# Second query tile's exponentials ahead of the first tile's fp16 copy, in a fused gated cross-attention and expert kernel

## The chip, the cores and the metric

One core of one Trainium2 chip runs the whole program. The metric is the device time of that core in microseconds. Before the change its median over 3 runs is 476.14 us (475.67 to 477.45).

## The reference

The program computes one transformer block over `x` (8 batches, 256 tokens, 128 channels) and a context of 512 tokens per batch. First comes a gated cross-attention with 16 heads of 64 channels:

```python
q = (xn @ w_q).reshape(B, SQ, NUM_HEADS, DIM_HEAD)
kv = context @ w_kv
scores = jnp.einsum('bqhd,bkhd->bhqk', q * SCALE, k)
attn = jax.nn.softmax(scores, axis=-1)
out = jnp.einsum('bhqk,bkhd->bqhd', attn, v).reshape(B, SQ, INNER)
x = x + jnp.tanh(g_xattn[0]) * (out @ w_out + b_out) * jnp.tanh(gate[0])
```

Then each token goes to the likeliest of 8 experts (at most 160 tokens each), which is a two-layer network of width 512 with a ReLU, and its output is added with a second gate. All inputs and outputs are float32.

## The kernel before

The attention is worked through in 64 steps, one for each batch `b` and pair of heads `hp` (8 batches of 8 pairs; `j = 8*b + hp` counts them). Heads of a pair lie side by side: a score bank holds 128 queries by two heads of 512 keys. The index `qt` (0 or 1) is the tile of 128 queries of the pair. `psAB` holds the scores of `qt` 0, `psCD` those of `qt` 1. There is one bank pair for each, used again by the next pair.

Every engine has its own program, written out in order; semaphores tie them. Nothing reorders the work at run time. For one pair the data goes this way:

- TensorE writes the scores of `qt` 0 and `qt` 1 (`scores`, lines 1234 and 1241). `scores(j, qt)` waits for the exponentials of pair `j-1` of the same `qt`, which free the bank.
- VectorE takes the row maximum of each tile (`row_max`, line 903) and makes of it the bias `NB` (line 906).
- ScalarE takes the exponentials (`exps`, line 752; two instructions, one for each head) from PSUM to the float32 tile `P32`.
- ScalarE copies `P32` to fp16, the high half of a split of each value in two (`phi`, line 762), into `PARTS`.
- GpSimd subtracts the high half from `P32` and writes the low half in fp16 (line 650).
- SyncE issues a DMA transpose of both halves of the tile, `PARTS` to `PT` (line 473), when GpSimd has finished that tile. There are two per pair, one for each `qt`.
- TensorE multiplies the transposed halves with the values of the heads (`values`, lines 1267 to 1269; 48 matmuls, the 24 of `qt` 0 first). It does so two steps later: in step `j` it works on pair `j-2`. VectorE then scales the result (lines 914 and 920).

In step `j` TensorE's order is: the scores of both tiles, the keys and queries of pair `j+2` (lines 1168 to 1170 into `psEF`), the transposes of pair `j-3`'s output (line 1278), what some steps have besides in the bank `psX` (projections, context and token transposes, router logits at line 1294), the values of pair `j-2`, and a block of the values' projection into `psX` (lines 1168 to 1170). That block's high half is copied out by ScalarE (`v_hi`, line 719) and its low half by VectorE (`v_lo`, line 896) in the next step, after the first row maximum; then `psX` is free.

ScalarE's order in a step is the one that the change touches: `exps` of `qt` 0; the copy of the next keys and queries (`kq_hi`, line 714; 3 of 8 steps have none); in single steps a further copy (`xt_copy` line 696 at `hp` 4, `tokt_copy` line 724 at `hp` 5, `v_hi` at `hp` 2); `phi` of `qt` 0; `exps` of `qt` 1; `ot_copy` (line 741); `phi` of `qt` 1; `v_hi`; in single steps a small copy or the router's exponentials.

SyncE's queue also carries loads between the transposes: a batch's context and tokens, 256 KB pieces of the experts' weights at `hp` 3 and 6, and one store of a batch's rows at `hp` 4.

After the 64 steps comes a tail of some 50 us with the last pairs and the experts.

Of the kernel before, what the change touches and what calls it, by code (L numbers as in the profile page):

```python
# [33 lines left out]
def gated_block(nc, x, ctx_1024, g_xattn, g_ffn, ln_gamma, ln_beta, w_q, w_kv, w_out, b_out, gate,  # L34
# [34 lines left out]
    with ExitStack() as ctx:  # L69
# [236 lines left out]
        def slots(b):  # L306

            for hp in range(PAIRS):
                yield b * PAIRS + hp, hp
# [5 lines left out]
        def is_last(b):  # L315
            return isinstance(b, int) and b == B - 1

        def is_first(b):
            return isinstance(b, int) and b == 0
# [6 lines left out]
        def v_group(b, hp):  # L326

            if hp >= PAIRS - 2:
                return None if is_last(b) else (b + 1, 0, hp - PAIRS + 2)
            return (b, 0, hp + 2) if hp < 2 else (b, 1, hp - 2)  # L330
# [4 lines left out]
        def ot_pair(j):  # L335

            return j - OT_BEHIND
# [25 lines left out]
        def next_pair(b, hp, k):  # L363

            return (b, hp + k) if hp + k < PAIRS else (b + 1, hp + k - PAIRS)
# [24 lines left out]
        def score_bank(qt):  # L390

            return psCD if qt else psAB
# [291 lines left out]
        def _(act):  # L684
# [5 lines left out]
            def xt_copy(b):  # L690

                act.wait_ge(xt_psum, b + 1)
                if b:

                    act.wait_ge(xt_lo_done, b)
                act.activation(XS[:], x_bank(b)[:, 0:SQ], ACT.Identity, bias=norm_q[:, 1:2],
                               scale=norm_q[:, 0:1]).then_inc(xt_f32, 1)

            def xt_hi(b):
                act.wait_ge(xt_f32, b + 1)  # L700
                act.activation(xT_hi[:, b % 2, :], XS[:], ACT.Copy).then_inc(xt_hi_done, 1)

            def ctxt_hi(b):
                act.wait_ge(ctxt_psum, b + 1)
                act.activation(cT_hi[:, b % 2, :], psX[:], ACT.Copy).then_inc(ctxt_hi_done, 1)

            def kq_hi(b, hp):
                j = b * PAIRS + hp
                if whole(j):
                    return  # L710
                act.wait_ge(kq_psum, j + 1)
                if ot_pair(j - AHEAD) >= 0:
                    act.wait_ge(ot_psum, ot_pair(j - AHEAD) + 1)
                act.activation(HL[:, hp % 2, H_KHI:H_KHI + KQ], kq_bank(j)[:, 0:KQ], ACT.Copy).then_inc(kq_hi_done, 1)  # L714

            def v_hi(b, half, kt, bank=psX):
                n = b * 2 * KT + half * KT + kt
                act.wait_ge(v_psum, n + 1)
                act.activation(VH[:, kt, 8 * half:8 * half + 8, 0:DH],  # L719
                               bank[:].rearrange("p (h d) -> p h d", d=DH), ACT.Copy).then_inc(v_hi_done, 1)  # L720

            def tokt_copy(b, bank=psX):
                act.wait_ge(tokt_psum, b + 1)
                act.activation(tT[:], bank[:, 0:QT * P], ACT.Copy).then_inc(tokt_done, 1)

            def router_exp(b):
                act.wait_ge(rstd_done, b + 1)
                act.wait_ge(route, b * ROUTE + 2)
                for q in range(QT):
                    last = act.activation(lexp[:, q, :], cand[:, q, :], ACT.Exp, scale=rstd[:, q:q + 1])  # L730
                last.then_inc(lexp_done, 1)

            def ot_copy(n, bank=psOT, pairs=1):

                b, pair = divmod(n, PAIRS)
                act.wait_ge(ot_psum, n + pairs)
                act.wait_ge(kq_done, min(n + OT_BEHIND + AHEAD + 1, LAST + 1))
                if b:

                    act.wait_ge(part_psum if pair < PAIRS // 2 else proj_psum, b)  # L740
                act.activation(OT[:, QT * pair:QT * (pair + pairs), :], bank.rearrange("p (t c) -> p t c", c=P),  # L741
                               ACT.Copy).then_inc(ot_done, pairs)

            def exps(b, hp, qt):
                j = b * PAIRS + hp
                par = hp % 2
                act.wait_ge(bias_done, 2 * j + qt + 1)
                if j >= 2:

                    act.wait_ge(plo_done, 2 * j - 4 + qt + 1)  # L750
                for h in range(2):
                    last = act.activation(P32[:, par, qt, SK * h:SK * h + SK], score_bank(qt)[:, SK * h:SK * h + SK],  # L752
                                          ACT.Exp, bias=NB[:, par, qt, h:h + 1])
                last.then_inc(exp_done, 1)

            def phi(b, hp, qt):
                j = b * PAIRS + hp
                act.wait_ge(exp_done, 2 * j + qt + 1)
                if j >= 2:

                    act.wait_ge(pt_in[qt][hp % 2], transposed_value(j - 2))
                act.activation(PARTS[:, hp % 2, qt, 0], P32[:, hp % 2, qt], ACT.Copy).then_inc(phi_done[qt], 1)  # L762
# [19 lines left out]
            def batch(b):  # L782
                for j, hp in slots(b):
                    if hp == CTX_STEP + 1 and not is_last(b):
                        ctxt_hi(b + 1)
                    exps(b, hp, 0)
                    if not (is_last(b) and hp + AHEAD >= PAIRS):
                        kq_hi(*next_pair(b, hp, AHEAD))
                    if hp == CTX_STEP:
                        v_hi(*v_group(b, hp))  # L790
                    if hp == X_STEP and not is_last(b):
                        xt_copy(b + 1)
                    if hp == TOKT_STEP and not is_first(b):
                        tokt_copy(b - 1)
                    if j < LAST:
                        phi(b, hp, 0)
                    exps(b, hp, 1)
                    if ot_pair(j) >= 0:
                        ot_copy(ot_pair(j))
                    if j < LAST:  # L800
                        phi(b, hp, 1)
                    if hp != CTX_STEP and v_group(b, hp):
                        v_hi(*v_group(b, hp))
                    if hp == X_STEP and not is_last(b):
                        xt_hi(b + 1)
                    if hp == LOGITS_STEP and not is_first(b):
                        router_exp(b - 1)

            each_batch(batch)
            for qt in range(QT):  # L810
                act.wait_ge(p_psum, qt + 1)
# [730 lines left out]
```

## Time and profile before

| | us |
|---|---|
| median of 3 runs | 476.14 |
| the profiled execution, its own time | 477.22 |
| its span | 475.4 |
| PE (TensorE) busy | 437.4 (92%) |
| ACT (ScalarE) busy | 386.3 (81%) |
| DVE (VectorE) busy | 360.6 (76%) |
| POOL (GpSimd) busy | 356.5 (75%) |

The profile shows one execution. Times in it are microseconds from the start of the span. An engine's row gives the start, the duration, the line of the kernel, what is written and read, and in brackets the idle time of the engine before it with what ended it. SPq is the queue of SyncE; a transpose's row there is the time of its issue, not that of its transfer. A row of the windows view gives the stretch, its length, the busy time of PE, PEld (TensorE's weight loads), DVE, ACT and POOL with the count of instructions, TensorE's granted clock, the DMA share and GB/s. A row of landing times gives the least, the median and the most from the issue of a transfer to its landing.

### The profile page before, as it was taken

The page shows a single profiled execution, that of the slowest core. Times are in us where ns is not written, and L with a number is a line of the kernel's source. Part 1 is how long each engine was busy: PE and PEld are TensorE (multiplying, and loading weights), DVE is VectorE, ACT ScalarE, POOL GpSimd, SP SyncE. Part 2 cuts the span into 40 slices and gives each one's busy share as a digit, 9 for nine tenths or more (in the row PEclk, how much of TensorE's full clock was granted, in tenths as well). Part 3 has the DMA queues.
Part 4 walks back from the last instruction along what each step waited for, and adds up shares of the span by engine and source line. Part 5 has one row for each costly group of instructions (what it writes and reads, how often), then busy time and mean ns, then how long its engine had stood idle before and what let it go on. Part 6 is the DMA issues. An engine that isn't in the chain of part 4 may idle for free.

```text
span 475.4 us, 13024 instructions
## 1 busy us (share of the span) xinstructions
PE 437.4 (92%) x5030; PEld 330.3 (69%) x5030; DVE 360.6 (76%) x789; ACT 386.3 (81%) x630; POOL 356.5 (75%) x270
## 2 busy tenths in 40 slices
PE   5789999999999999999999999999999899987793
PEld 3466667776777766776777677767687577766793
DVE  4678887778887897889777888789788777893522
ACT  4789988899988998899889998899889889881230
POOL 3677886888878887898788887888789787851225
PEclk9899999999999999999999999999999999999799
DMA  5399999899999999999999999999999979993201
GB/s 169 147 145 207 213 188 188 170 181 196 194 193 209 193 195 203 168 218 212 188 184 196 200 200 174 212 182 202 186 172 167 185 155 163 146 192 100 58 11 44
DMA packets 283036, 82.08 MB, mean 173 GB/s; under 512 B 264387, under 2 KB 280435, under 8 KB 282976
## 3 DMA queue, kind: packets, MB, share of 16 engines
q1 hardware_dynamic: 281600, 77.96, 93.0%
q0 software_dynamic: 1376, 3.30, 2.1%
q8 instruction: 40, 0.66, 0.6%
q14 instruction: 20, 0.16, 0.1%
HBM read 10.83 MB, written 5.14 MB: 34 GB/s over the span
## 4 chain that ended last, share of the span: by engine, by line
PE 45%; DVE 20%; ACT 15%; issue 8%; DMA 6%; POOL 4%; POOLq 0%; another core or an unknown queue 0%; SPq 0%; ACTq 0%; DVEq 0%
DVE MXL L903 8%; ACT P L752 7%; DMA PT<-PARTS 5%; PE psAB L1234 4%; PE psAB L1241 4%; DVE HL L890 3%; POOL PARTS L650 3%; ACT HL L714 3%; PE psO L1267 3%; PE psX L1319 3%; PE psCD L1241 3%; ACT PARTS L762 3%; PE psO L1269 3%; PE psX L1355 3%; PE psO L1268 3%
## 5 line engine op out<-in xcount | busy, mean ns | idle before, releaser
L650 POOL TENSOR_TENSOR PARTS<-P,PARTS 128x1024 f16<-128x1024 f32 x125 | 267.4, 2144 | 61.1 <-ACT PARTS L762 59.7
L762 ACT ACTIVATE PARTS<-P 128x1024 f16<-128x1024 f32 x126 | 136.0, 1080 | 0.8 <-DMA PT<-PARTS 0.2
L752 ACT ACTIVATE P<-psAB,NB 128x512 f32<-128x512 f32 x128 | 81.6, 694 | 39.2 <-DVE NB L906 38.7
L903 DVE TENSOR_REDUCE MXL<-psAB 128x2 f32<-128x1024 f32 x64 | 78.3, 1224 | 40.4 <-PE psAB L1241 23.2
L1267 PE MATMUL psO<-VH,PT 128*128 128x65 f16 x1008 | 98.4, 194 | 3.8 <-DMA PT<-PARTS 3.1
L1268 PE MATMUL psO<-VL,PT 128*128 128x64 f16 x1008 | 98.3, 192 | 0.0
L1269 PE MATMUL psO<-VH,PT 128*128 128x65 f16 x1008 | 98.2, 193 | 0.0
L1267 PEld LDWEIGHTS psO<-VH,PT 128*128 128x128 f16 x1008 | 92.0, 98 | 7.2 <-DMA PT<-PARTS 3.8
L1268 PEld LDWEIGHTS psO<-VL,PT 128*128 128x128 f16 x1008 | 91.3, 98 | 0.5
L1269 PEld LDWEIGHTS psO<-VH,PT 128*128 128x128 f16 x1008 | 91.4, 97 | 0.0
L752 ACT ACTIVATE P<-psCD,NB 128x512 f32<-128x512 f32 x128 | 81.7, 703 | 0.1
L903 DVE TENSOR_REDUCE MXL<-psCD 128x2 f32<-128x1024 f32 x64 | 77.7, 1214 | 0.2 <-PE psCD L1241 0.2
L896 DVE TENSOR_TENSOR VL<-psX,VH 128x512 f16<-128x512 f32 x63 | 43.1, 684 | 8.7 <-ACT VH L719 8.5
L890 DVE TENSOR_TENSOR HL<-psEF,HL 128x768 fp32r<-128x768 f32 x41 | 39.2, 957 | 7.7 <-ACT HL L714 4.2
L1241 PE MATMUL psCD<-HL 64*128 64x512 f32 x252 | 38.1, 407 | 5.9 <-ACT P L752 5.8
L1241 PE MATMUL psAB<-HL 64*128 64x512 f32 x252 | 41.2, 432 | 2.0 <-ACT P L752 2.0
L719 ACT ACTIVATE VH<-psX 128x512 f16<-128x512 f32 x63 | 39.3, 624 | 0.0
L714 ACT ACTIVATE HL<-psEF 128x768 fp32r<-128x768 f32 x41 | 33.3, 813 | 2.7 <-PE psEF L1170 2.5
L741 ACT ACTIVATE OT<-psEF 128x256 f32<-128x256 f32 (+1 forms) x63 | 26.1, 414 | 11.5 <-PE psEF L1278 8.4
L1168 PEld LDWEIGHTS psEF<-cT_hi,w_hi 128*128 128x128 f32 x63 | 11.9, 189 | 32.8 <-issue 31.1
L1241 PEld LDWEIGHTS psCD<-HL 64*128 64x128 f32 x252 | 23.1, 187 | 16.1 <-ACT P L752 11.7
L1168 PE MATMUL psEF<-cT_hi,w_hi 128*128 128x512 f32 x63 | 32.0, 508 | 1.3 <-DVE cT_lo L877 1.3
(208 smaller groups left out, 865.0 us busy)
## 6 DMA issues: line engine op xcount, KB each, us to landing
ctx_raw<-in_ctx_dram SPq DMA_DIRECT2D x8, 256.0 KB, 3.6
w1s<-in_L_ffn_w_dram SPq DMA_DIRECT2D x8, 256.0 KB, 3.9
w2s<-in_L_ffn_w_dram SPq DMA_DIRECT2D x8, 256.0 KB, 3.5
PT<-PARTS SPq DMA_TRANSPOSE x126, 5.2
experts_table<-zeros POOLq DMA_DIRECT2D x2, 645.0 KB
X<-in_x_dram SPq DMA_DIRECT2D x8, 128.0 KB, 3.0
wraw<-in_L_xattn_w_kv_dram SPq DMA_DIRECT2D x4, 256.0 KB, 4.7
out_dram<-row SPq DMA_DIRECT2D x8, 128.0 KB, 2.7
```

Of the source, the lines that this page charges most:

```text
L650: pool.tensor_tensor(PARTS[:, par, qt, 1], P32[:, par, qt], PARTS[:, par, qt, 0], ALU.subtract).then_inc(plo_done, 1)
L714: act.activation(HL[:, hp % 2, H_KHI:H_KHI + KQ], kq_bank(j)[:, 0:KQ], ACT.Copy).then_inc(kq_hi_done, 1)
L752: last = act.activation(P32[:, par, qt, SK * h:SK * h + SK], score_bank(qt)[:, SK * h:SK * h + SK], ACT.Exp, bias=NB[:, par, qt, h:h + 1])
L762: act.activation(PARTS[:, hp % 2, qt, 0], P32[:, hp % 2, qt], ACT.Copy).then_inc(phi_done[qt], 1)
L890: dve.tensor_tensor(hl[:, H_KLO:H_KLO + KQ], kq_bank(j)[:, 0:KQ], hl[:, H_KHI:H_KHI + KQ].bitcast(F32), ALU.subtract).then_inc(kq_done, 1)
L896: dve.tensor_tensor(VL[:, kt, 8 * half:8 * half + 8, :], bank[:].rearrange("p (h d) -> p h d", d=DH), VH[:, kt, 8 * half:8 * half + 8, 0:D ...
L903: dve.tensor_reduce(MXL[:, par, qt, :, 0], score_bank(qt)[:].rearrange("p (h n) -> p h n", h=2), AX.X, ALU.max, negate=True).then_inc(max_ ...
L1168: pe.matmul(dst, hi_l, hi_r, start=True, stop=False)
L1241: last = pe.matmul(score_bank(qt)[:, SK * h:SK * h + SK], hl[rows, q + P * qt:q + P * qt + P], hl[rows, k:k + SK], start=(q == H_QHI and k ...
L1267: pe.matmul(psO[:, g:g + DH + 1], phi, VH[:, kt, head, 0:DH + 1], start=first_, stop=False)
L1268: pe.matmul(psO[:, g:g + DH], phi, VL[:, kt, head, :], start=False, stop=False)
L1269: last = pe.matmul(psO[:, g:g + DH + 1], plo, VH[:, kt, head, 0:DH + 1], start=False, stop=last_)
```

## The change

In each step but the last, ScalarE's program has `exps` of `qt` 1 ahead of `phi` of `qt` 0, and not behind it. Nothing else is changed: the same instructions with the same operands, semaphores and waits.

```diff
                     if hp == TOKT_STEP and not is_first(b):
                         tokt_copy(b - 1)
+                    exps(b, hp, 1)
                     if j < LAST:
                         phi(b, hp, 0)
-                    exps(b, hp, 1)
                     if ot_pair(j) >= 0:
                         ot_copy(ot_pair(j))
```

## Rows read from the trace of the kernel before

**Rows 1.** The page's busy time, share of span and instructions of each engine.

```profile
PE 437.4 (92%) x5030; PEld 330.3 (69%) x5030; DVE 360.6 (76%) x789; ACT 386.3 (81%) x630; POOL 356.5 (75%) x270
```

**Rows 2.** Busy time by windows: the pair steps, and the fifth batch alone.

```profile
18.00:425.00 407.00, 389.30 (x4623) 287.82 (x4624) 331.40 (x698) 364.63 (x588) 331.99 (x231) 0.99 1.07 189
...
222.90:274.60 51.70, 50.66 (x617) 37.67 (x614) 42.62 (x93) 46.34 (x75) 43.56 (x32) 1.00 1.10 193
```

**Rows 3.** Waits of TensorE's matmuls, 18 to 425 us: total, times, longest.

```profile
PE psCD L1241 <- ACT P L752: 5.8, 11, 1.2
PE psX L1186 <- DVE VL L896: 4.4, 7, 0.7
PE psO L1267 <- DMA PT<-PARTS: 3.1, 6, 1.3
```

**Rows 4.** Waits of all engines, and of SyncE's queue, whole span.

```profile
POOL PARTS L650 <- ACT PARTS L762: 59.7, 83, 3.4
ACT P L752 <- DVE NB L906: 38.7, 41, 2.2
...
SPq L473 <- POOL PARTS L650: 179.9, 90, 17.6
```

**Rows 5.** ScalarE in order of time, fifth batch, pair hp 4.

```profile
251.48 1.07 ACT L762 ACTIVATE PARTS<-P 128x1024 f16<-128x1024 f32 x1
252.43 1.28 ACT L752 ACTIVATE P<-psCD,NB 128x512 f32<-128x512 f32 x2
253.57 0.42 ACT L741 ACTIVATE OT<-psEF 128x256 f32<-128x256 f32 x1
253.83 1.10 ACT L762 ACTIVATE PARTS<-P 128x1024 f16<-128x1024 f32 x1
```

**Rows 6.** VectorE in order of time: the same pair's second bias.

```profile
250.91 0.16 DVE L906 TENSOR_REDUCE NB<-MXL 128x2 f32<-128x4 f32 x1
```

**Rows 7.** GpSimd in order of time: the same pair's two low halves.

```profile
252.64 2.15 POOL L650 TENSOR_TENSOR PARTS<-P,PARTS 128x1024 f16<-128x1024 f32 x1 [1.23 <-ACT PARTS L762]
255.01 2.15 POOL L650 TENSOR_TENSOR PARTS<-P,PARTS 128x1024 f16<-128x1024 f32 x1 [0.23 <-ACT PARTS L762]
```

**Rows 8.** SyncE's queue in order of time, fifth batch, ahead of hp 4's transposes.

```profile
252.05 1.74 SPq L455 DMA_DIRECT2D w2s<-in_L_ffn_w_dram  x2
254.81 5.60 SPq L473 DMA_TRANSPOSE PT<-PARTS  x2
```

**Rows 9.** Line 473: landing of transposes issued 249 to 263.3 us.

```profile
DMA to landing us min/median/max: 4.4/4.4/6.2
```

**Rows 10.** TensorE in order of time: values of hp 4, before and after its second tile's start.

```profile
263.03 0.19 PE L1269 MATMUL psO<-VH,PT 128*128 128x65 f16 x1
263.25 0.20 PE L1267 MATMUL psO<-VH,PT 128*128 128x65 f16 x1
```

**Rows 11.** Line 473 at 211.9 us (fourth batch, hp 5, second tile), and TensorE's first matmul on it.

```profile
L473 SPq DMA_TRANSPOSE PT<-PARTS x1: 3372/3372/3372, 211.9 to 211.9; - x1
...
DMA to landing us min/median/max: 5.3/5.3/5.3
...
217.31 0.19 PE L1267 MATMUL psO<-VH,PT 128*128 128x65 f16 x1
```

**Rows 12.** ScalarE and VectorE in order of time, fifth batch, hp 5 into hp 6.

```profile
256.71 0.45 ACT L724 ACTIVATE tT<-psX 128x256 f32<-128x256 f32 x1
256.97 1.13 ACT L762 ACTIVATE PARTS<-P 128x1024 f16<-128x1024 f32 x1
...
260.27 0.70 ACT L719 ACTIVATE VH<-psX 128x512 f16<-128x512 f32 x1
...
257.31 0.16 DVE L906 TENSOR_REDUCE NB<-MXL 128x2 f32<-128x4 f32 x1
...
261.14 0.68 DVE L896 TENSOR_TENSOR VL<-psX,VH 128x512 f16<-128x512 f32 x1
```

**Rows 13.** TensorE in order of time: router logits of hp 6, fifth batch.

```profile
261.87 0.61 PE L1294 MATMUL psX<-gw_mid,tT 128*128 128x8 f32 x4
```

## The prediction

> **What bounds the kernel now.** I read the busy shares first [rows 1]: PE 92%, ACT 81%, POOL 75%. Then the windows [rows 2]: in the fifth batch, a full turn of eight pairs, PE's matmuls fill 50.66 of 51.70 us with the clock granted in full, while ACT has 5.4 us free and POOL 8.1. So in a steady batch TensorE leaves about 1 us open. The reader is to see that little can be won there, whatever ACT does. Then PE's own waits [rows 3]: of 407 us, 5.8 us in 11 waits are for the exponentials that free `psCD`. 4.4 us are for `v_lo` and 3.1 us for transposed tiles. Last, the other engines' waits [rows 4]: POOL waits 59.7 us in 83 places for the fp16 copy, and SyncE's queue waits 179.9 us in 90 places for POOL (17.6 of it is one wait). So `phi`, the low half, the transpose and the values form a chain with little slack, each link starting when the one before ends.
>
> The Trainium skill (Perfetto Trace Analysis, Identifying the Most-Contended Engine) says that matmul busy time is a poor measure of room on TensorE and that weight-load time is the better one. By that, 37.67 of 51.70 us is taken in the fifth batch and TensorE has room. The waits above disagree: they list almost no time in which it stood.
>
> **What the change adds and removes.** No instruction is added or removed; 63 steps have two neighbours swapped, no DMA and no queue entry moves.
>
> *The gain: earlier `exps` of `qt` 1.* At hp 4 ACT's further copy gives way to `phi` at 251.48 and `exps` starts at 252.43 [rows 5]. Its bias was ready at 250.91 + 0.16 = 251.07 [rows 6]. Swapped, `exps` starts at 251.48, 0.95 us earlier. What it is worth is what PE waits for it: at most 5.8 us [rows 3], about half of it in the first batch, the rest some 0.25 us a batch at one pair and 1.1 us in the last batch. Elsewhere PE is not ready for the scores of `qt` 1 any earlier, so the gain is zero.
>
> *The cost: later `phi` of `qt` 0, and what hangs on it.* `phi` starts after two exponentials. They take 253.57 − 252.43 = 1.14 us from start to the next instruction's start [rows 5], so `phi` moves from 251.48 to 252.62. POOL's first low half was released by `phi` after 1.23 us idle [rows 7], so it moves from 252.64 to 253.78 and ends at 255.93. `phi` of `qt` 1 keeps its time, 253.83, for the sum ahead of it is the same. POOL's second low half started at 255.01; now it can start only at 255.93, and ends at 258.08 instead of 257.16: 0.92 us late. So both tiles are late, the first by 1.14 and the second by 0.92 us, although only one copy moved.
>
> The two transposes are issued from 254.81, when the first low half ends (252.64 + 2.15 = 254.79), and the queue had been free since 252.05 + 1.74 = 253.79 [rows 8]. The lateness passes through: 255.95 and 258.1. They land up to 6.2 us after issue [rows 9]. Now who waits: the values of hp 4 run without a gap to 263.03, and the second tile's first matmul starts at 263.25 instead of 263.06 [rows 10]. PE had already caught up with the transfer: slack zero. At hp 5 of the fourth batch a transpose issued at 211.9 lands 5.3 us later, at 217.2, and is used at 217.31 [rows 11]: slack 0.1. Six waits for transposed tiles in 62 pairs [rows 3] say that most other pairs have theirs in time.
>
> Per batch there is then one delay of the lateness less the slack. Once TensorE is late, the following pairs' scores are late too, so the same microsecond isn't paid twice in that batch, but the next batch pays again, as the lateness is measured from the pair's own scores. The lateness is 1.14 and 0.92 us, so about 1.0. I take all of it for the fifth to seventh batches (slack zero), 0.95 for the fourth, and 0.7 for the second and third, whose slack I put at 0.3 as an estimate above the 0.1 of the fourth: 5.35 us. Bounds of the lateness that reaches PE, per batch: 0, if the transfer engines had a backlog when the transpose came; 1.25, if the second tile is held up as much as the first and its issue comes late besides. I take the value near the top, since the queue was free when the first transpose came [rows 8].
>
> The skill (DMA: Bandwidth & Descriptors, Latency and other measured facts) gives 261 GB/s for one kernel's DMA transposes. An estimate from that page is 2.0 us for a tile of 512 KiB, so two tiles would take 4.0 us of a pair's 6.4 and a late one would be caught up before use. No run here shows that spare time: landing takes 4.4 to 6.2 us [rows 9].
>
> *ACT now waits in three of eight steps.* Where no `kq_hi` stands between (hp 5, 6, 0), the second bias isn't ready when `exps` of `qt` 1 comes. At hp 5 the copy ahead gives way at 256.97, the bias comes at 257.31 + 0.16 = 257.47 [rows 12]. Before, `phi` lay in that gap. Now ACT idles 0.5 us, and `phi` of `qt` 1 and `v_hi` come 0.5 us later: `v_hi` ends at 261.5 rather than 260.97. `v_lo` started at 261.14 [rows 12], now at 261.5, and router logits, which need its bank, started at 261.87 [rows 13], right after it (261.14 + 0.68 = 261.82). They move by 0.35 us. That is a delay ahead of the same values of hp 4, so it is inside the 1.0 us. The same at hp 0, where `ot_copy` was held up anyway, should cost about 0.13 us in each of six batches: 0.8 us. At the end, the last-but-one pair (hp 6) passes its 0.6 us on to the last exponentials and from there to the tail; I take 0.7, between 0 and 0.9.
>
> *First and last batch.* In the first, PE gains near 2 us at its early pairs, but the values there follow the landings by 0.5 to 1 us, and by nothing at hp 4 and 5, so the gain is spent within a few pairs: 0, between −2 and +1. In the last, the gain of 1.1 meets 0.6 of lateness: −0.5. The 0.25 us gained in each middle batch comes just ahead of the wait for the transposed tile and is lost in it: 0.
>
> **Sum.** 5.35 + 0.8 + 0.7 + 0 − 0.5 = 6.35 us. I take a fifth off the 5.35 and the 0.8 for transfers that catch up: 5.1 us. The profiled execution took 477.22 us, so 482.3 in its place. It lies 1.08 above the median of the three runs, so the predicted time is 476.14 + 5.1 = 481.2 us.
>
> **The rivals.**
>
> *Faster: PE's wait is what counts.* Place: the scores of `qt` 1. The 5.8 us [rows 3] go, and the late tiles are caught up because the transfer engines were backlogged when they came. It decides where the lateness that reaches the values stays below the slack plus 0.25 us. For it: the waits are real, and each load of 256 KB ahead of a transpose could hide lateness. Against it: the queue was empty for 1 us before the critical transpose [rows 8], and five of those waits are only 0.25. With 1 to 2 us lost at the tail it gives 476.14 − 4.3 = 471.8. The rule on weight-load time belongs here. Chance 0.10.
>
> *No change.* Transfers absorb all but 0.2 us a batch (1.2), the losses at hp 0 and tail are 1.5, the gains outside the middle batches 2: 476.14 + 0.7 = 476.8. For it: PE waits for a transposed tile only six times before the change [rows 3], and some of the lateness falls into the time in which the queue is loaded anyway. The page's transfer rate would mean this one. Chance 0.23.
>
> *Much slower: ACT or POOL becomes the chain.* The idle stretches of ACT (0.5, 0.6 and 0.9 us at hp 5, 6 and 0) are all passed on, 2.0 us in each of seven batches, beside a part of the above: 476.14 + 14 = 490. Against it: ACT waits 38.7 us for the first bias in 41 places [rows 4], so it has room to catch up, 5.4 us in a batch [rows 2]. Chance 0.09.
>
> **Chances and range.** Forecast 0.58, no change 0.23, faster 0.10, much slower 0.09. The forecast's own range is 478 to 485. To hold 8 in 10 I go to 474.8 below and 485.8 above, which takes most of the no-change case. A measurement of this kernel tells about 0.5% (2.4 us) from nothing. Slower by more than that: 0.09 and nearly all of 0.58, so 0.66; within it 0.23; faster 0.11.
>
> **What would show each step.** In the profile after: PE's waits `psCD` <- ACT nearly gone; ACT idle before `exps` of `qt` 1 at hp 5, 6 and 0 (a new row of waits for the bias, in `psCD`'s form); POOL's two low halves back to back, with no idle before the second; the first transpose issued about 1.1 us later from the pair's first exponentials; PE's waits for the transposed tiles up from 3.1 us to about 8, one at hp 4 or 5 of each batch; a batch of 51.3 to 52.9 us grown by about 1. The prediction is wrong if the landing times, measured from the pair's scores, don't move, or if they move and TensorE doesn't wait. It is wrong in size if waits come at more than one pair of a batch, or if `v_lo` gates TensorE more than the transposes do.

## Result: 2.8% slower, more than twice the forecast loss

The changed kernel takes 489.88 us in the median of 6 runs (487.83 to 494.11); the kernel before, beside it, 476.79 us (475.67 to 480.98). The ratio is 1.0276, 95% interval 1.0239 to 1.0312, so 13.1 us are lost. The forecast was 481.2 us with a range to 485.8: the sign was right, the size wrong.

The profiled execution took 492.89 us with a span of 491.0, against 477.22 and 475.4. First the page's busy line, which answers to [rows 1], then its line on the chain that ended last, by engine.

```profile
PE 436.6 (89%) x5030; PEld 332.8 (68%) x5030; DVE 362.8 (74%) x789; ACT 385.7 (79%) x630; POOL 355.5 (72%) x270
```

```profile
POOL 53%; issue 25%; PE 10%; DMA 5%; ACT 3%; DVE 3%; POOLq 1%; SPq 0%; ACTq 0%; DVEq 0%
```

The same line before:

```profile
PE 45%; DVE 20%; ACT 15%; issue 8%; DMA 6%; POOL 4%; POOLq 0%; another core or an unknown queue 0%; SPq 0%; ACTq 0%; DVEq 0%
```

No instruction was added, and TensorE's busy time even fell from 437.4 to 436.6 us. All of the loss is idle time. Before, TensorE led the chain with 45%; now GpSimd does, with 53%. That share is no measure of the loss: in e5 below, which loses 2.6 us, GpSimd still leads with 39%. TensorE's waits over the whole program, the changed kernel (answer to [rows 3]):

```profile
PE psO L1267 <- DMA PT<-PARTS: 12.3, 16, 1.6
...
PE psX L1186 <- DVE VL L896: 3.9, 6, 0.7
PE psX L1286 <- DVE VL L896: 3.0, 6, 0.5
PE psX L1294 <- DVE VL L896: 3.0, 7, 1.4
PE psX L1333 <- issue: 3.0, 1, 3.0
PE psCD L1241 <- ACT P L752: 2.3, 3, 0.8
PE psX L1319 <- DVE VL L896: 1.8, 6, 0.6
PE psX L1168 <- DVE VL L896: 1.8, 2, 0.9
...
PE psAB L1241 <- ACT P L752: 1.5, 1, 1.5
```

Before, beside the waits of [rows 3]:

```profile
PE psAB L1241 <- ACT P L752: 2.0, 1, 2.0
...
PE psX L1294 <- DVE VL L896: 1.1, 1, 1.1
...
PE psAB L1308 <- ACT P L752: 0.9, 1, 0.9
```

Together they make a balance. Waits for transposed tiles: 3.1 to 12.3, +9.2. Waits for `v_lo`: 4.4 + 1.1 = 5.5 before; now the 13.5 of the five rows above and 1.1 in three smaller ones (L1365, L1302, L1333), 14.6, so +9.1. The ranks (L1333, the places of the tokens within their experts), 0.2 to 3.0, +2.8. Waits for the exponentials (`psCD`, `psAB`): 5.8 + 2.0 + 0.9 and a last one of 0.2 before, 8.9, and 3.8 now, −5.1. Together +16.0, beside 15.6 us of span. So the wait that the change attacks did shrink, and two others grew by more than three times as much.

How one batch grew: ScalarE's first exponentials of the fifth and the sixth batch, first the kernel before, then the changed one.

```profile
221.61 0.69 ACT L752 ACTIVATE P<-psAB,NB 128x512 f32<-128x512 f32 x1
...
273.35 0.69 ACT L752 ACTIVATE P<-psAB,NB 128x512 f32<-128x512 f32 x1
```

```profile
232.41 0.69 ACT L752 ACTIVATE P<-psAB,NB 128x512 f32<-128x512 f32 x1 [0.73 <-DVE NB L906]
...
286.05 0.69 ACT L752 ACTIVATE P<-psAB,NB 128x512 f32<-128x512 f32 x1 [1.50 <-DVE NB L906]
```

51.74 us became 53.64. Read the same way, the seven full batches took 50.0, 51.3, 51.3, 51.3, 51.7, 52.1 and 52.9 before, and 54.9, 53.4, 53.0, 53.0, 53.6, 53.1 and 53.7 after. The six batches in the middle grew by 9.1 us together. From the last batch's hp 6 to the end it was 58.6 and is 60.1. TensorE's waits for transposed tiles in those six batches, before (67.75 to 378.40 us) and then in the changed kernel (73.09 to 392.79 us):

```profile
PE psO L1267 <- DMA PT<-PARTS: 2.1, 4, 1.3
```

```profile
PE psO L1267 <- DMA PT<-PARTS: 7.4, 11, 1.6
```

In the same stretches the waits for `v_lo` went from 3.9 to 10.3 us and those for the exponentials from 1.5 to 0.

Now the pair that the prediction followed, hp 4 of the fifth batch, in the changed kernel: ScalarE, which answers to [rows 5].

```profile
262.21 1.28 ACT L752 ACTIVATE P<-psCD,NB 128x512 f32<-128x512 f32 x2
263.35 1.09 ACT L762 ACTIVATE PARTS<-P 128x1024 f16<-128x1024 f32 x1
264.30 0.42 ACT L741 ACTIVATE OT<-psEF 128x256 f32<-128x256 f32 x1
264.56 1.10 ACT L762 ACTIVATE PARTS<-P 128x1024 f16<-128x1024 f32 x1
```

GpSimd at hp 4 and at hp 5, which answers to [rows 7]:

```profile
264.52 4.24 POOL L650 TENSOR_TENSOR PARTS<-P,PARTS 128x1024 f16<-128x1024 f32 x2 [1.44 <-ACT PARTS L762]
...
270.52 4.24 POOL L650 TENSOR_TENSOR PARTS<-P,PARTS 128x1024 f16<-128x1024 f32 x2 [0.27 <-ACT PARTS L762]
```

The two low halves now stand in one row, back to back. Measured from the pair's own first exponentials (249.19 before, 259.92 after), the first starts 4.60 us in instead of 3.45, and the second ends at 8.84 instead of 7.97: late by 1.15 and 0.87, as worked out. What SyncE's queue makes of it (answer to [rows 8]):

```profile
263.86 1.64 SPq L455 DMA_DIRECT2D w2s<-in_L_ffn_w_dram  x2
266.69 6.32 SPq L473 DMA_TRANSPOSE PT<-PARTS  x2
273.06 0.58 SPq L444 DMA_DIRECT2D out_dram<-row  x1
273.74 5.62 SPq L473 DMA_TRANSPOSE PT<-PARTS  x2
```

The same queue before, in which the last row is hp 5's first transpose:

```profile
260.45 0.58 SPq L444 DMA_DIRECT2D out_dram<-row  x1
261.13 2.87 SPq L473 DMA_TRANSPOSE PT<-PARTS  x1
```

hp 5's first transpose went from 261.13 − 255.57 = 5.56 us after its own exponentials to 273.74 − 266.30 = 7.44: late by 1.88, although GpSimd had its tile only 1.2 late. hp 4's two issues held the queue until 273.01, the store until 273.64. And TensorE, at the second tile of the values of hp 4 and of hp 5 (answer to [rows 10]):

```profile
274.47 0.20 PE L1267 MATMUL psO<-VH,PT 128*128 128x65 f16 x1 [0.19 <-DMA PT<-PARTS]
...
281.74 0.20 PE L1267 MATMUL psO<-VH,PT 128*128 128x65 f16 x1 [1.48 <-DMA PT<-PARTS]
```

The wait forecast at hp 4 is small; the large one is a pair later. The fifth batch is one of the two with the largest wait at hp 5. In the six middle batches the second tile of hp 5 is waited for every time, by 0.40 to 1.64 us, that of hp 4 by 0.19 to 0.39 us in four of the six, and one of hp 6 once. GpSimd delivers both tiles of hp 5 about 1.2 us late in all six; the queue then issues the first 0.7 to 1.9 us late.

### The profile page after: what moved, and what is told of

Its sections match the earlier page's. It is cut to its first block, busy times and chain, and to the rows that moved or that the text cites. A ratio compares the mean times of both kernels' runs of the same rounds, so it can differ in the third digit from the quotient of the medians.

```text
span 491.0 us, 13024 instructions
## 1 busy us (share of the span) xinstructions
PE 436.6 (89%) x5030; PEld 332.8 (68%) x5030; DVE 362.8 (74%) x789; ACT 385.7 (79%) x630; POOL 355.5 (72%) x270
## 3 DMA queue, kind: packets, MB, share of 16 engines
q1 hardware_dynamic: 281600, 77.96, 91.1%
## 4 chain that ended last, share of the span: by engine, by line
POOL 53%; issue 25%; PE 10%; DMA 5%; ACT 3%; DVE 3%; POOLq 1%; SPq 0%; ACTq 0%; DVEq 0%
POOL PARTS L650 41%; DMA PT<-PARTS 4%; POOL XN L543 2%; POOL experts_table L615 2%; PE psEF L1479 2%; POOL row L593 2%; POOL xT_lo L548 1%; POOL X L629 1%; DVE MXL L903 1%; PE psX L1488 1%; PE psO L1488 1%; POOL rstd L588 1%; POOL rstd L536 1%; ACT PARTS L762 1%; ACT P L752 1%
## 5 line engine op out<-in xcount | busy, mean ns | idle before, releaser
L762 ACT ACTIVATE PARTS<-P 128x1024 f16<-128x1024 f32 x126 | 134.4, 1070 | 0.0
L1267 PE MATMUL psO<-VH,PT 128*128 128x65 f16 x1008 | 100.8, 195 | 12.9 <-DMA PT<-PARTS 12.3
L1267 PEld LDWEIGHTS psO<-VH,PT 128*128 128x128 f16 x1008 | 92.8, 99 | 17.6 <-DMA PT<-PARTS 13.2
L1268 PE MATMUL psO<-VL,PT 128*128 128x64 f16 x1008 | 100.6, 193 | 0.0
L1269 PE MATMUL psO<-VH,PT 128*128 128x65 f16 x1008 | 100.5, 194 | 0.0
L752 ACT ACTIVATE P<-psCD,NB 128x512 f32<-128x512 f32 x128 | 81.5, 693 | 16.8 <-DVE NB L906 16.8
L1268 PEld LDWEIGHTS psO<-VL,PT 128*128 128x128 f16 x1008 | 92.3, 99 | 0.5
L1241 PE MATMUL psCD<-HL 64*128 64x512 f32 x252 | 36.3, 392 | 2.3 <-ACT P L752 2.3
L1168 PE MATMUL psX<-w_hi,cT_hi 128*128 128x512 f32 x63 | 30.7, 488 | 2.7 <-DVE VL L896 1.8
L1241 PEld LDWEIGHTS psAB<-HL 64*128 64x128 f32 x252 | 20.5, 185 | 17.0 <-issue 10.3
```

The lines of the kernel that those rows point to most:

```text
L1168: pe.matmul(dst, hi_l, hi_r, start=True, stop=False)
L1241: last = pe.matmul(score_bank(qt)[:, SK * h:SK * h + SK], hl[rows, q + P * qt:q + P * qt + P], hl[rows, k:k + SK], start=(q == H_QHI and k ...
L1267: pe.matmul(psO[:, g:g + DH + 1], phi, VH[:, kt, head, 0:DH + 1], start=first_, stop=False)
L1268: pe.matmul(psO[:, g:g + DH], phi, VL[:, kt, head, :], start=False, stop=False)
L1269: last = pe.matmul(psO[:, g:g + DH + 1], plo, VH[:, kt, head, 0:DH + 1], start=False, stop=last_)
```

## The experiments

Intervals are 95% intervals of the ratio to the kernel before; microseconds lost are the ratio's excess over 1 times 477. Code added to or taken from a kernel shifts its line numbers (the wait at L1267 above stands at L1271 or L1265 below); the tile names tell the rows. A profile shows one execution, so lengths of batches in it are weaker evidence than the ratios.

### The swap in parts

Four kernels have the swap at some pairs only. This is e1's edit of the changed kernel; e2 has `hp not in (4, 5)`, e9 `hp in (2, 3)`, e10 `hp in (6, 7, 0, 1)`:

```diff
-                    exps(b, hp, 1)
+                    early = hp in (4, 5)
+                    if early:
+                        exps(b, hp, 1)
                     if j < LAST:
                         phi(b, hp, 0)
+                    if not early:
+                        exps(b, hp, 1)
```

**e1, hp 4 and 5.** 

> The swap at pairs hp 4 and 5 alone, in all eight batches. Theory A (the late phi of qt 0 makes GpSimd's two low halves, the transposes and so the values of hp 4 and 5 late, and TensorE waits for each of them): it holds what the middle batches lost, 1.3 us each beside most of what the first lost, so 484 to 488 us. Theory B (ScalarE idle before the second bias at hp 5, 6 and 0 is passed on by v_hi and v_lo): only one of its three places is here, so 478 to 480. Theory C (the loss is spread over all pairs): a quarter of it, about 480.

**e2, all but hp 4 and 5.** 

> The swap at all pairs but hp 4 and 5. Theory A: the tiles of the other pairs land 1 us or more before their use and TensorE doesn't wait for them, so the middle batches keep their time; what is left is the first batch's early pairs and the tail (hp 6's late low half holds up the mark of the experts and the ranks), 477 to 480 us. Theory B: two of three idle places are here, 484 or more. Theory C: three quarters of the loss, about 486.

**e9, hp 2 and 3.** 

> The swap at pairs hp 2 and 3 alone. Their own tiles land 1.4 us or more before use, and ScalarE has no idle time before the second bias there. If lateness is carried on by GpSimd, SyncE's queue and the transfers to the next pairs (theory A with carry), the waits appear at hp 4 and 5 and it costs 3 to 6 us: 480 to 483. If each tile is late by itself alone, nothing but the first batch's early pairs is left, 477 to 478.5.

**e10, hp 6, 7, 0 and 1.** 

> The swap at pairs hp 6, 7, 0 and 1 alone. With carry, the lateness of these pairs meets slacks of 1.4 to 6 us at hp 7, 0, 1 and 2 and should be spent there in the middle batches; left are ScalarE's idle time at hp 6 and 0, the first batch's first two pairs and the tail: 3 to 5 us, 480 to 482. If the parts added up to the whole 13 us, with 7.1 at hp 4 and 5, this would be the rest that hp 2 and 3 don't cost.

| swap at | ratio | interval | us lost |
|---|---|---|---|
| e1: hp 4, 5 | 1.0151 | 1.0104 to 1.0197 | 7.2 |
| e9: hp 2, 3 | 1.0099 | 1.0065 to 1.0132 | 4.7 |
| e10: hp 6, 7, 0, 1 | 1.0091 | 1.0055 to 1.0127 | 4.3 |
| e2: all but 4, 5 | 1.0233 | 1.0158 to 1.0307 | 11.1 |
| all | 1.0276 | 1.0239 to 1.0312 | 13.2 |

No group of pairs is free. The parts don't simply add up: e1, e9 and e10 make 16.2 us together, e1 and e2 18.3 (give or take 4), where the whole swap costs 13.2, so some of the cost seems to be shared. e1's time fits the theory of late tiles, but its waits don't single them out:

```profile
PE psO L1271 <- DMA PT<-PARTS: 5.7, 11, 2.2
```

That is 2.6 us more than before, while its waits for `v_lo` are 11.7 against 5.5. e2 flatly contradicts the theory's first form: pairs whose tiles land with time to spare cost 11 us. e10's time is as expected, but not its account: its waits for tiles are 9.0 us, at hp 4 to 6 but for one of 2.1 in the first batch, so the lateness isn't all spent in the slack. e9 shows why. Its waits of TensorE:

```profile
PE psO L1271 <- DMA PT<-PARTS: 9.3, 12, 1.8
```

They stand at hp 4 to 6 for the most part, where this kernel's order is the old one. In its sixth batch hp 4's low half of qt 0 is in time on GpSimd:

```profile
307.95 2.14 POOL L650 TENSOR_TENSOR PARTS<-P,PARTS 128x1024 f16<-128x1024 f32 x1 [0.28 <-ACT PARTS L762]
```

SyncE's queue there, and then TensorE's start on hp 5's second tile:

```profile
303.57 5.63 SPq L473 DMA_TRANSPOSE PT<-PARTS  x2
309.24 1.58 SPq L455 DMA_DIRECT2D w2s<-in_L_ffn_w_dram  x2
310.92 7.06 SPq L473 DMA_TRANSPOSE PT<-PARTS  x2
...
318.71 10.64 SPq L473 DMA_TRANSPOSE PT<-PARTS  x4
```

```profile
327.47 0.20 PE L1271 MATMUL psO<-VH,PT 128*128 128x65 f16 x1 [1.85 <-DMA PT<-PARTS]
```

Compare the kernel before at the same place, GpSimd and then SyncE's queue:

```profile
304.24 2.15 POOL L650 TENSOR_TENSOR PARTS<-P,PARTS 128x1024 f16<-128x1024 f32 x1 [1.23 <-ACT PARTS L762]
```

```profile
304.38 1.58 SPq L455 DMA_DIRECT2D w2s<-in_L_ffn_w_dram  x2
306.41 6.07 SPq L473 DMA_TRANSPOSE PT<-PARTS  x2
...
313.20 8.51 SPq L473 DMA_TRANSPOSE PT<-PARTS  x3
```

The low half ends 5.6 us after the pair's first exponentials in both (304.50 and 300.79). But its transpose is issued 5.62 us after them before, when the low half ends, and 6.42 in e9, when hp 3's late transposes and the loads behind them have left the queue. One pair on it is 6.03 before (313.20 − 307.17) and 7.83 in e9 (318.71 − 310.88). Lateness passes down the queue, and grows there. This batch shows the largest case. At hp 4 of the six middle batches the kernel before issues the first transpose 0.03 us after its low half each time; e9 does so 0.2 to 0.8 us after it in five of them, and in the seventh batch, where the queue has fewer loads, at once.

### Only the first batch, and all but the last

**e3, the swap where `j < PAIRS`.** 

> The swap in the first batch alone. By the two profiles the first batch is 4.9 us longer after the change, which I had put at 0: if that comes from the swap in it, 480 to 482 us. If it came from where the granted clock happened to fall in that profile, the time is within 1 us of before, 476 to 478.

479.23 us, ratio 1.0040 (1.0010 to 1.0069): 1.9 us, between the two expectations. Its profiled first batch took 54.9 us like the changed kernel's. But in e14 below, whose order in the first batch is that of the kernel before, that batch took 51.5 in its profile, not 50.0, and in e7 51.9. With the swap in it the profiles have 54.9, 54.9, 54.0, 54.0 and 51.9 (changed kernel, e3, e11, e13, e6). One profile doesn't hold the first batch's length to better than 2 to 3 us; the means are 51.1 and 53.9.

**e11, the swap where `b < B - 1`.** 

> The swap in all batches but the last. The tail of the profile after was 1.5 us longer than before: GpSimd's late low half of the last but one pair holds up the marking of the experts, the ranks on TensorE and with them the last transposes. If that is the swap's doing, 1.5 to 3 us come back: 487 to 488.5. Otherwise it stays at 489 to 490.

489.77 us, ratio 1.0255 (1.0194 to 1.0315): 1.0 us came back in the ratio, whose interval is 2.9 us to either side. Inconclusive for the tail. The wait of 3.0 us for the ranks (L1333) is gone from its list, so that wait is the swap's doing. The profiles of the other runs say more. From the last batch's hp 6 to the end, kernels whose last batch has the order of the kernel before take 57.0 (e1), 56.3 (e3), 57.1 (e4), 56.7 (e7), 57.0 (e8), 57.5 (e9), 57.3 (e11) and 57.0 us (e12); the 58.6 of the kernel before is the longest of them. With the swap there it is 60.1 (changed kernel), 60.9 (e2), 59.2 (e10) and 59.0 (e6). The tail costs some 2.5 to 3 us, an estimate from these profiles, and not the 1.5 of the first pair of them.

### Late tiles without touching ScalarE, and ScalarE's order without late tiles

**e4, one added instruction on GpSimd.** 

> The kernel before, ScalarE's order untouched, with one added GpSimd instruction of about 1.1 us (a sum of 448 columns into a spare tile) ahead of the low half of qt 0 at hp 4 and 5. It makes the transposed tiles as late as the swap does there (1.1 and 0.9 us) and leaves ScalarE alone. Theory A: near the time of the swap at hp 4 and 5 alone, 483 to 487 us. Theory B: no loss, 476 to 478.

```diff
...
+                        if qt == 0 and hp in (4, 5):
+                            if b or hp > 4:
+                                pool.wait_ge(spare_done, 2 * b + hp - 4)
+                            pool.tensor_tensor(spare[:, 0:448], P32[:, par, qt, 0:448], P32[:, par, qt, 0:448],
+                                               ALU.add).then_inc(spare_done, 1)
                         pool.tensor_tensor(PARTS[:, par, qt, 1], P32[:, par, qt], PARTS[:, par, qt, 0],
                                            ALU.subtract).then_inc(plo_done, 1)
```

The lines left out make the spare tile and its semaphore. 482.96 us, ratio 1.0101 (1.0065 to 1.0136): 4.8 us, just under the range of theory A. Lateness of the tiles alone, with ScalarE as before, costs two thirds of what the swap costs at the same pairs (e1, 7.2). Its waits:

```profile
PE psO L1274 <- DMA PT<-PARTS: 10.9, 13, 1.9
```

**e5, the changed kernel with a shorter low half.** 

> The changed kernel, with GpSimd's low half of qt 0 made for the first head of the pair only (512 of 1024 columns; the second head's low half of that tile is left at zero, so that part of the computation is left out). The GpSimd instruction then takes about 1.1 us instead of 2.1 and the tile is as early as before the change, ScalarE's order stays the changed one. Theory A (late tiles, carried on by GpSimd and SyncE's queue): most of the loss is gone, 477 to 481 us. Theory B (ScalarE idle before the second bias, passed on by v_hi and v_lo): the loss stays, 487 to 490.

```diff
...
+                        n = 2 * SK if qt else SK
-                        pool.tensor_tensor(PARTS[:, par, qt, 1], P32[:, par, qt], PARTS[:, par, qt, 0],
+                        pool.tensor_tensor(PARTS[:, par, qt, 1, 0:n], P32[:, par, qt, 0:n], PARTS[:, par, qt, 0, 0:n],
                                            ALU.subtract).then_inc(plo_done, 1)
...
```

The lines left out have VectorE set the unused low half to zero at the start. 480.24 us, ratio 1.0054 (1.0018 to 1.0090): 2.6 us are left of 13.2. GpSimd's two low halves of hp 4 in the fifth batch, and then ScalarE's first exponentials of that pair:

```profile
255.26 3.36 POOL L654 TENSOR_TENSOR PARTS<-P,PARTS 128x512 f16<-128x512 f32 x2 [2.33 <-ACT PARTS L766]
```

```profile
250.65 1.27 ACT L756 ACTIVATE P<-psAB,NB 128x512 f32<-128x512 f32 x2 [1.50 <-DVE NB L910]
```

The second low half ends 258.62 − 250.65 = 7.97 us in, the figure of the kernel before to the hundredth. ScalarE's order is the changed one. Its waits:

```profile
PE psO L1272 <- DMA PT<-PARTS: 5.3, 10, 1.1
PE psX L1191 <- DVE VL L900: 4.4, 7, 0.7
PE psX L1291 <- DVE VL L900: 3.3, 7, 0.5
PE psX L1299 <- DVE VL L900: 3.1, 7, 1.4
...
PE psX L1324 <- DVE VL L900: 1.8, 6, 0.6
```

The waits for `v_lo` are all still there, as in the changed kernel (14.7 us in all, against its 14.6). The 2.6 us (0.9 to 4.3) are what they cost less what the shorter waits for the exponentials give back. So about 10.6 of the 13.2 us hang on late tiles. This is the run that decides between the theories. Two things it doesn't separate. The edit also takes about 1 us of work from GpSimd in every pair, and the kernel before wasn't run with that same edit at all pairs (e12 has it at four of eight). And in the six middle batches alone the split is more even: they are 3.8 us longer than before in e5's profile, 9.1 in the changed kernel's.

### Is it the loads in the queue?

**e6 and e7, the experts' loads moved**, in the changed kernel and in the one before.

```diff
-        PIECES = {3: 2, 6: 1}
+        PIECES = {0: 0, 1: 1, 7: 2}
...
```

> The changed kernel, with the 256 KB loads of the experts' weights moved in SyncE's queue from hp 3 (two) and 6 (one) to hp 0, 1 and 7 (one each), where the transposes have slack. If lateness is carried from pair to pair by a queue that has no room from hp 3 to hp 6 (theory D), 3 to 6 us come back: 484 to 487. If each tile is late by itself alone (theory A without the queue), the waits at hp 4 and 5 stay and it is 488 to 490.

> The kernel before with the same loads moved. It has 3.2 us of waits for transposed tiles, most of them in the sixth and seventh batches; theory D says that they go and it is 473 to 476 us. Without theory D it is within 1 us of before, 476 to 478.

e6: 488.41 us, ratio 1.0264 (1.0171 to 1.0357). e7: 477.37 us, 1.0004 (0.9971 to 1.0037). No gain can be told in either, though e6's interval is too wide to rule out the 3 us of its expectation. In e6 the waits for tiles are 11.2 us in 20 places; they moved, in part to hp 0 to 3, at and behind the places where the loads now are.

**e13 and e14, the loads taken out of the pair steps** and issued behind them, in the changed kernel and in the one before.

> The changed kernel with all sixteen 256 KB loads of the experts' weights taken out of the pair steps and issued after them, ahead of the experts (which adds some 10 to 20 us of waiting to the tail, the same as in the kernel before with the same edit). What counts is the difference to that kernel. If the transfer queue's lack of room carries the lateness from pair to pair, the difference shrinks from 13 us to 8 or less and the waits for transposed tiles in the middle batches fall from about 1.4 us a batch to under 0.7. If GpSimd's two low halves in a row carry it, the difference stays at 11 to 14.

> The kernel before with the same edit, as the base for the last one. Its waits for transposed tiles (3.1 us, in the last batches with loads) go to near 0 if the loads make them, so its pair steps take 2 to 3 us less; its time as a whole is 485 to 495 for the later loads.

e13: 498.49 us, 1.0419 (1.0353 to 1.0484). e14: 487.32 us, 1.0200 (1.0144 to 1.0255). The difference of the medians is 11.2 us. Their waits for tiles, e13 first:

```profile
PE psO L1265 <- DMA PT<-PARTS: 8.1, 12, 1.8
```

```profile
PE psO L1265 <- DMA PT<-PARTS: 3.7, 5, 1.4
```

Without the loads the swap adds 4.4 us of these waits, with them 9.2. So about half of the added waits go with the loads. But the difference in time shrank by only 2 us of 13, at the edge of what these runs tell, so my expectation of 8 or less failed, and so did that of under 0.7 us of these waits in a middle batch (it is 0.8). The waits for `v_lo` are as long as in the changed kernel (14.5 us). The waits in the sixth and seventh batches did not go in e14 either (they are 2.9 of its 3.7 us), so the loads don't make them. In the kernel before, it is the landing that is long there: the second tile of hp 5 lands 6.0 and 6.4 us after its issue, against 4.6 to 5.3 in the four batches ahead. What makes it long is open.

One rival stays untested. By the profiles' pages, the packets of the queue that these transfers go through take 93.0% of the 16 transfer engines' span before and 91.1% after. Whether an issue holds the queue long by itself, or because the transfer engines behind it are busy, no run here separates.

### The other direction

**e8, the copy of keys and queries behind `phi` of `qt` 0 at hp 4 and 7**, in the kernel before: `phi` comes 0.7 us earlier.

```diff
-                    if not (is_last(b) and hp + AHEAD >= PAIRS):
+                    later = hp in (4, 7)
+                    ahead = not (is_last(b) and hp + AHEAD >= PAIRS)
+                    if ahead and not later:
                         kq_hi(*next_pair(b, hp, AHEAD))
...
                     if j < LAST:
                         phi(b, hp, 0)
+                    if ahead and later:
+                        kq_hi(*next_pair(b, hp, AHEAD))
                     exps(b, hp, 1)
```

> The kernel before with ScalarE's copy of the next keys and queries behind phi of qt 0 at hp 4 and 7 instead of ahead of it: the opposite of the change, phi of qt 0 comes 0.7 us earlier there. Theory A: the tiles of hp 4 and, through the queue, of hp 5 land 0.5 to 0.7 us earlier and the waits for them shrink, 473.5 to 476 us. Against it: the copy's low half on VectorE waits 0.9 us longer and holds up the scaling of the output, then 477 to 479.

480.52 us, ratio 1.0054 (1.0022 to 1.0087): slower by 2.6 us. Waits for tiles fell from 3.1 to 2.3 us, and those for the exponentials rose from 5.8 to 8.9 at line 1241 of the kernel before. The waits for `v_lo`, which VectorE makes, rose as well, from 5.5 to 7.5. The counter-argument of the expectation held, by its sign; whether by the scaling of the output, as it says, I didn't trace.

**e12, the kernel before with the low half of `qt` 0 at hp 2 to 5 made for one head only.** 

> The kernel before, with GpSimd's low half of qt 0 at hp 2, 3, 4 and 5 made for the first head of the pair only (the second head's low half keeps what an earlier pair left, so that part of the computation is left out). The tiles come 1 us earlier than before. The reverse of the change's effect: if the time hangs on the tiles' lateness alike in both directions, 3 us are won at most, since that is all that TensorE waits for them: 474 to 476. If nothing moves, TensorE's own work is the bound in the kernel before.

475.29 us, ratio 0.9978 (0.9944 to 1.0012): no difference that can be told. Its waits for tiles are 4.3 us, not fewer than the 3.1 before. The run makes only the first tile of a pair early; the low half of the second, for which TensorE mostly waits, ends when it did (7.97 us after the first exponentials at hp 4). So it says that an earlier first tile wins nothing sure, and nothing of an earlier second one. Tiles 1 us later lose 5 to 10 us (e4, and e5 against the changed kernel). No version here beats the kernel before for certain.

## Why the prediction was wrong in size

**Right: what moves, and by how much.** `exps` of `qt` 1 earlier, `phi` late by 1.14, the low halves late by 1.14 and 0.92, back to back: the trace has 1.15 and 0.87. The idle time of ScalarE before the second bias at hp 5 came too, and `v_lo` made the logits of hp 6 late. The waits for the exponentials shrank by 5.1 us, and as forecast the gain was lost again, though at another place: TensorE, early at hp 5, waits 0.5 us for `v_lo` before the token transposes (L1286, in each of six batches), not for the tile.

**Right in its sum, partly by luck: the late tiles of the middle batches.** The term was 5.35 us for six batches, and the waits for tiles there grew from 2.1 to 7.4, by 5.3. The swap at hp 4 and 5 alone (e1) makes these batches 5.9 us longer in its profile. But the term had one delay of 1.0 us, at hp 4 of the fifth batch, and 0.7 in the second and third for a slack that was guessed. The waits stand mostly at hp 5, whose two tiles come 1.2 us late from GpSimd and then find a queue that hp 4's tiles and the store still hold: 1.88 us late at issue in the fifth batch.

**Failed: the other pairs' lateness put at nothing.** That "most other pairs have theirs in time" was the step, read from six waits for transposed tiles before. I took it as a sign that lateness elsewhere is spent in the slack between landing and use. e9 and e2 show that it isn't: it leaves the pair by the queue, not by the tile, and what I called hidden was hidden only for the pair itself. The six middle batches grew by 9.1 us, where the sum had 5.35 + 0.8, and 4.9 after the discount. "The same microsecond isn't paid twice in that batch" holds in part: e1 and e2 cost more one by one (18.3 us) than together (13.2), a difference just clear of their intervals. But the following pairs don't just shift along.

**Failed: 0 for the first batch.** e3 has 1.9 us there (0.5 to 3.3). Its middle lies outside the bound of +1, its interval doesn't.

**Mis-sized: the tail and `v_lo`.** For the tail I had 0.7; the profiles of the runs put it at some 2.5 to 3 us. Nothing was put down for the ranks: at the last batch's hp 6, `phi` comes after 0.92 us of ScalarE's idle time and the exponentials of `qt` 1, GpSimd marks the experts behind that tile's low half, and TensorE stands 3.0 us. `v_lo` at hp 0 and 1 was put at 0.13 us a batch; the wait at L1319 is up to 0.6. The waits for it before were 5.5 us, not the 4.4 of the one row that I read, and over the program they now exceed those for tiles (14.6 against 12.3). That was one of the signs named for an error in size; waits at more than one pair of a batch was the other, and it came too.

**The rivals.** The time is that of "much slower" (490), its mechanism isn't. That rival passed ScalarE's idle time on, and e5, which keeps it (17.6 us before the second exponentials, 16.8 in the changed kernel), loses 2.6 us, not 13. "No change" counted on the same slack, and its chance of 0.23 was too high. The discount for "transfers that catch up" had the wrong sign.

**Room on TensorE.** The "faster" rival gave the waits for the exponentials their worth and had the late tiles caught up. It fell: 5.1 us less of such waits went with 13 us more in all. The Trainium skill (Perfetto Trace Analysis, Identifying the Most-Contended Engine) takes weight-load time as a better measure of room on TensorE than matmul busy time; by it, with 330.3 of 475.4 us before, there would have been much room to catch up. The trace disagrees, and it decides: in the fifth batch before, TensorE's matmuls left 1.0 of 51.7 us open.

**Time to catch up on the queue.** Two issues in a row hold SyncE's queue for 5.6 to 7.1 us in the rows above and 5.1 us in the mean of the whole program (321.8 us for 126 of them), and a pair step takes about 6.4. With the loads, the issues fill 41 to 49 us of each middle batch before, of 51 to 53. The Trainium skill (DMA: Bandwidth & Descriptors, Latency and other measured facts) gives 261 GB/s for one kernel's DMA transposes, by which an estimate is 2.0 us for a tile and 4.0 for two, with time to spare in a pair. The rows disagree, and they decide.

## What to carry to other kernels

Before moving work that feeds an in-order queue later, add up how long that queue is held by a round of its entries; if it is near the round's length, lateness at any entry is paid further down, and the slack at the entry's own consumer says nothing. Follow a delayed tile to the next round's issue, not only to its use. And where the bound engine waits for several things in turn, relief at one can be collected at the next: look at what it waits for next before counting a gain. Count a producer's waits over all its rows, and read a length that rests on one profile against other profiles of the same order.

## What the hardware showed that I had not expected

The same DMA transpose of the same tile takes between 1.3 and 4.3 us to issue on SyncE's queue; the sum over 126 of them is 321.8 us before and 322.3 after. The time is not spread by pair in any way that I could tie to a cause.

TensorE's granted clock fell in the changed kernel's first batch, behind two waits for tiles of 1.2 and 0.7 us at hp 4. A window of the changed kernel, with the granted clock as the last figure but two:

```profile
61.70:65.00 3.30, 3.30 (x29) 2.55 (x31) 0.61 (x2) 1.85 (x4) 2.98 (x2) 0.50 1.12 215
```

For 3.3 us it is at the lower level, 1.2 GHz; from 60.0 to 61.6 and from 65.1 to 67.0 us it is 1.00. The kernel before has such a stretch of its own around the start of the pair steps:

```profile
17.00:26.00 9.00, 5.96 (x21) 3.90 (x21) 6.89 (x14) 7.01 (x11) 6.20 (x7) 0.62 0.38 150
```

The changed kernel shows 1.00 in that window, and TensorE's busy time is 0.8 us less in it over the whole program. So in this pair of profiles the clock explains none of the loss as a whole. In the tail it has a small part: from the last batch's hp 6 on, the mean granted clock is 0.92 before and 0.89 after, and TensorE's busy time 43.16 and 43.90 us.
